# A four-stage transformer pipeline on one core: job 0's turn, the conditions and the table of places set anew

## What is computed

```python
# block 0: x += gate * self_attention(rope) ; x += gate * cross_attention ; x += gate * mlp(gelu)
mod = cond_global @ adaLN_W + adaLN_b                  # shifts, scales, gates
x_norm = _ln(x, norm1_w) * (1 + sc_msa) + sh_msa
q1, k1, v1 = qkv(x_norm[:, :n]); q2, k2, v2 = qkv(x_norm[:, n:])   # q, k turned by rope
self_out = _attn(q, k, v, attn_mask) @ attn_out_W
x = x + g_msa * self_out
...
# block 1: x += attention(ada_ln(x), ada_ln(ctx)) ; block 2: self attention, cross attention, mlp
# block 3: softmax attention over ctx, a router over three experts (silu), a gate, and the sum
```

## Time and profile before

| what | value |
|---|---|
| median of three runs | 637.37 us |
| the profiled execution, its own time | 639.46 us |
| its span | 637.7 us |
| PE busy | 560.0 us, 88% |
| DVE busy | 443.4 us, 70% |
| ACT busy | 407.7 us, 64% |
| POOL busy | 219.6 us, 34% |
| mean granted TensorE clock | 0.985 |

### The profile page before, as it was taken

How to read it: one execution, slowest core, us unless ns; L and a number is a source line. 1 busy time by engine, 2 the same in 40 slices (tenths; PEclk the granted TensorE clock), 3 DMA queues, 4 the chain that set the end, 5 groups by cost and what they waited for, 6 DMA issues and landing times.

```text
span 637.7 us, 25649 instructions
## 1 busy us (share of the span) xinstructions
PE 560.0 (88%) x11216; PEld 318.0 (50%) x11216; DVE 443.4 (70%) x1157; ACT 407.7 (64%) x704; POOL 219.6 (34%) x324
## 2 busy tenths in 40 slices
PE   6688977998779978898888988899999999998997
PEld 2344434445435545454544654465455655575456
DVE  5779877767896668768886878688676786244213
ACT  3233634675677447874788476868898868656762
POOL 6512442443541443523463344534342332110000
PEclk9999998999999979999998999999999999999999
DMA  6802000000000000000000000000000000000000
GB/s 207 320 4 68 20 2 19 19 2 20 19 20 3 20 1 21 17 3 19 21 18 2 5 18 18 2 20 4 19 4 2 4 3 19 4 3 19 3 3 35
DMA packets 15349, 16.32 MB, mean 26 GB/s; under 512 B 1830, under 2 KB 13108, under 8 KB 14856
## 3 DMA queue, kind: packets, MB, share of 16 engines
q1 hardware_dynamic: 14664, 10.70, 5.4%
q10 hardware_dynamic: 576, 4.00, 1.7%
HBM read 13.60 MB, written 1.09 MB: 23 GB/s over the span
## 4 chain that ended last, share of the span: by engine, by line
PE 56%; ACT 23%; DVE 13%; issue 5%; SPq 1%; POOL 1%; DMA 0%; DVEq 0%; POOLq 0%; ACTq 0%
PE lin L1027 17%; ACT P L639 14%; PE big L1027 11%; PE big L1190 9%; PE avp L1215 8%; PE big L1169 3%; DVE mhl L867 3%; PE big L1197 3%; ACT xn L603 2%; ACT L639 2%; PE lin L1119 1%; ACT L648 1%; ACT hid L648 1%; PE mtp L1027 1%; ACT hid L673 1%
## 5 line engine op out<-in xcount | busy, mean ns | idle before, releaser
L867 DVE TENSOR_REDUCE mhl<-big 128x8 bf16<-128x616 f32 (+1 forms) x160 | 149.4, 962 | 48.8 <-PE big L1169 46.7
L570 POOL TENSOR_TENSOR qm<-qT,hm 128x512 f32<-128x512 f32 x80 | 85.6, 1071 | 92.2 <-PE big L1197 49.8
L639 ACT ACTIVATE P<-big 128x1024 f32<-128x1024 f32 x64 | 62.0, 1021 | 69.4 <-PE big L1197 69.2
L1190 PE MATMUL big<-qm,kT 32*128 32x512 f32 x640 | 94.5, 661 | 0.0
L1215 PE MATMUL avp<-P,Vp 128*32 128x128 f32 x2560 | 90.4, 283 | 0.0
L556 POOL TENSOR_TENSOR kbm<-kT,hm 128x308 bf16<-128x308 f32 (+1 forms) x80 | 70.0, 874 | 51.0 <-PE big L1169 32.2
L533 POOL TENSOR_SCALAR rstd<-mv 128x4 f32<-128x4 f32 (+3 forms) x37 | 8.7, 234 | 218.6 <-DVE mv L816 218.3
L639 ACT ACTIVATE P<-big,padcol 128x1024 f32<-128x1024 f32 x64 | 67.8, 1110 | 25.0 <-PE big L1197 24.9
L1215 PEld LDWEIGHTS avp<-P,Vp 128*32 128x32 f32 x2560 | 71.8, 113 | 20.1 <-issue 17.2
L1027 PE MATMUL lin<-hT,W 128*32 128x512 f32 (+2 forms) x608 | 77.6, 589 | 0.2
L1169 PE MATMUL big<-kbm,qb 32*128 32x308 bf16 (+1 forms) x320 | 50.9, 332 | 23.0 <-ACT P L639 22.6
(11 more groups left out here) (208 smaller groups left out, 878.4 us busy)
## 6 DMA issues: line engine op xcount, KB each, us to landing
gring<-gate_rows SPq DMA_DIRECT2D x20, 256.0 KB, 3.2
W<-in_w ACTq DMA_DIRECT2D x2, 1152.0 KB, 14.0
hid<-in_ws SPq DMA_DIRECT2D x2, 768.0 KB, 5.8
W<-in_w ACTq DMA_DIRECT2D x1, 1088.0 KB, 9.1
x<-in_x SPq DMA_DIRECT2D x4, 256.0 KB, 6.8
out<-x SPq DMA_DIRECT2D x4, 256.0 KB, 2.4
ctx<-in_ctx SPq DMA_DIRECT2D x4, 154.0 KB
ctxT<-in_ctxT SPq DMA_DIRECT2D x4, 154.0 KB
```

Of the source, the lines that this page charges most:

```text
L570: nc.gpsimd.tensor_tensor(qm[:, j % 2], q.broadcast_to([128, 4, T]), mask.broadcast_to([128, 4, T]), ALU.mult).then_inc(qm_ready, 1)
L639: nc.scalar.activation(P[:, 8 * half:8 * half + 8, :], big[:, 2 * half:2 * half + 2, :].rearrange("p g (h q) -> p (g h) q", h=4), ACT.Exp, ...
L867: v.tensor_reduce(mhl[:].rearrange("p (g c) -> p g c", c=32)[:, 2 * half:2 * half + 2, 0:4], big[:, 2 * half:2 * half + 2, 0:4 * kw].rearr ...
L1190: mm(big[:, g, :].rearrange("p (h q) -> p h q", h=4), kT[s][r, b * kw:b * kw + 128], qm[r, j % 2], start=(a > 0), stop=False, skip_group_c ...
```

## The change

Of the table `SLOTS`, two of 45 rows are shown as samples; the others move by a few slots in the same manner, and the number and kind of units stay.

```diff
 SLOTS = {
...
-    (1, 0): [0, 3, 6],
+    (1, 0): [6, 7, 12],
...
-    (6, 0): [18],
+    (6, 0): [28],
...
-UNITS = ([("B", u, 0) for u in FIRST] + [("START", None, None)]
-         + [("B", u, 0) for u in (("p0", "k"), ("p0", "q"), ("p0", "v"))])
+UNITS = ([("B", u, 0) for u in FIRST] + [("START", None, None), ("B", ("p0", "k"), 0), ("A", 0, 0),
+                                         ("B", ("p0", "q"), 0), ("B", ("p0", "v"), 0)])
 for _slot in range(END):
-    UNITS.append(("A", _slot // 4, _slot % 4))
+    if _slot > 0:
+        UNITS.append(("A", _slot // 4, _slot % 4))
     UNITS += [("B", u, s) for slot, u, s in PLACED if slot == _slot]
-EARLY = [8, 12, 6, 6]
+EARLY = [8, 7, 2, 6]
...
                 v.tensor_scalar(sinT[:], sinT[:], turnsign[:], None, ALU.mult).then_inc(sign_set, 1)
+                v.tensor_scalar(mqk[:], mqk8[:], -1.0, BIG, ALU.add, ALU.mult)
+                v.tensor_scalar(mkq[:], mkq8[:], -1.0, BIG, ALU.add, ALU.mult).then_inc(masks_ready, 1)
+
+            def later_constants():
+
                 v.tensor_tensor(condr[:], condT[:].unsqueeze(2).broadcast_to([128, B, 3]),
                                 rw[:, 2:3, :].broadcast_to([128, B, 3]), ALU.mult)
-                for dst, src in ((mqk, mqk8), (mkq, mkq8), (mcb[:, 0:B * C], mc8)):
-                    i = v.tensor_scalar(dst[:], src[:], -1.0, BIG, ALU.add, ALU.mult)
-                chain(i)
-                v.memset(mhl[0:1, 0:1], 0.0).then_inc(consts_ready, 1)
+                v.tensor_scalar(mcb[:, 0:B * C], mc8[:], -1.0, BIG, ALU.add, ALU.mult).then_inc(consts_ready, 1)
...
             for kind, u, s in UNITS:
                 if kind == "START":
+                    later_constants()
                     for half in range(2):
                         maxima(0, half)
+                    turned(0)
                 elif kind == "A":
                     if s == 0:
-                        turned(u)
-                    if s == 0:
                         if u > 0:
+                            turned(u)
                             normalise(u - 1)
...
                 if part == "mods":
                     pe.wait_ge(silu_done, 1)
                     pe.wait_ge(ws_rest_in, 32)
+                    pe.wait_ge(consts_ready, 1)
...
                 if kind == "START":
                     keep_warm(EARLY[3])
-                    pe.wait_ge(consts_ready, 1)
+                    pe.wait_ge(masks_ready, 1)
```

More of the change, by code:

```diff
@@ L389, in build @@
             "cond_in", "ws_first_in", "ws_rest_in", "ident_in", "consts_in", "w_first_in", "w_rest_in"))
-        first_mods, consts_ready = sem("first_mods"), sem("consts_ready")
+        first_mods, masks_ready, consts_ready = sem("first_mods"), sem("masks_ready"), sem("consts_ready")
         gate_rows_out = sem("gate_rows_out")
```

## The result

| | before | changed |
|---|---|---|
| median of four runs each, same chip | 639.53 us (637.12 to 641.99) | 632.38 us (630.35 to 633.42) |
| ratio, 95% interval | | 0.9891 (0.9848 to 0.9934) |
| profiled execution, span | 639.46, 637.7 | 630.35, 628.5 |
| PE busy, mean granted clock | 560.0, 0.985 | 553.0, 0.993 |

What follows compares the result with a forecast made beforehand. It took PE and each job's own path to bound the kernel from job 4 on. Start 3.5 plus table 0.5 gave 4.0 us off 639.46: 635.5, expected as 633.4 for a run, range 629.3 to 638.0.

Steps and rivals of the forecast that it cites:

- Constants, 0.2 us by the lock: Set-up: condr and mcb leave the chain ahead of sample 0's rope but wait for GpSimd's qm; gain 0.2 us, bounds 0.2 to 0.85.
- Job 0's turn, job 1's copy at 28.9: First jobs: job 0's copy of turned maxima at 19.2 us instead of 23.89, job 1's at 28.9 instead of 36.76.
- The stall: PE's 3.34 us idle inside the conditions' matmuls, read as instructions delayed behind the weights; it goes in the new order.
- Conditions, job 2's copy at 40.4: Conditions and their tables now ahead of job 2's copy, uncovered; that copy at 40.4 us, 4.5 us earlier than before.
- Bias rows, cost 1.3 (0 to 1.8): On DVE behind job 3's copy: their 1.8 us partly fill 0.5 us of idle time, costing 1.3 us.
- First gates, "it just fits": SP's first gate loads behind the bias rows: land at 60.0 us, first used at 60.4; a miss costs its lateness.
- Start, 3.5 us: Set-up and first jobs together: 3.2 us earlier at job 4's copy, 3.5 us with the next window's lost copy of V.
- Table, 0.5 us: Moved units in jobs from 4 on: 0.5 us gained, an even shift of 5% of PE's 54 us idle being 2.7 us.
- The rival with this result (628.5): Table gives more than the start: PE's idle time in jobs 4 to 79 shrinks by a tenth, 5.4 us; chance 0.22.
- the absorbed gain: Rival: stall tied to the conditions returns 3.3 us and bias rows cost their full 1.8; 636.7 us, chance 0.15.
- The slower one: Rival: the granted clock falls several times before job 4, adding 5 us; 638.4 us, chance 0.08.
- Its own signs: Listed trace marks for right (five copy times, no long stall) and wrong (clock under 0.9, distance growing to 8 or 0).

Runs made afterwards that it cites:

- The experiment: Changed kernel with condr and mcb one step later on DVE, behind job 0's turned copy and k's rope: ratio 0.9864, median 631.9 us.
- start and conditions: Changed set-up and the conditions at slots 6, 7 and 12, other table rows as in the kernel before: 639.91 us, ratio 0.9991 to the kernel before.
- the table alone: Changed kernel's whole new table, conditions included, with the set-up of the kernel before: 635.53 us, ratio 0.9935 to the kernel before.
- the start alone: Changed set-up (UNITS, constants, EARLY) with the whole table of the kernel before: 638.58 us, ratio 0.9968 to the kernel before.

## Why the prediction was right, and where it was not

- *Idle matmuls, gain nothing:* right in total. In the trace above the clock did fall at 12.7 us, and the scores' mask took 1.04 us for 0.62, so the maxima waited 0.28 us for PE behind mcb; with the old idle matmuls job 0's copy came no earlier (19.15). (The counts go from 18 to 9, not from 20 to 11.)
- *Constants, 0.2 us by the lock:* 0.1 and 0.4 in the two traces, with condr stretched from 0.20 to 1.04. The experiment shows both sides: behind k's rope the whole gain is there (0.94). The bounds of 0.2 to 0.85 held nearly.
- *Job 0's turn, job 1's copy at 28.9:* 29.07 and 28.73.
- *The stall:* the reading as instructions that came late was right: it was tied to a count (twice shown), and its end came 1.3 us behind the packet's landing. That the weights held the packet up is not shown. "The stall then goes" was right for its 3.34 us. Missed: the next multiple, 962, gives a pause of 1.2 to 1.6 us in the same stretch, since PE runs the conditions' 256 records faster than the next packet comes; its 0.9 us on the gate rows lie in job 2's window.
- *Conditions, job 2's copy at 40.4:* 40.64 and 39.96.
- *"From job 2 to job 3 nothing else changes (9.68 us)":* failed. It took 10.47 us in both traces of the changed kernel, 0.8 more. All of it is DVE's wait for PE's k projection behind job 2's turn, and it comes with the moved conditions: 10.47 with start and conditions and with the table alone as well, 9.68 with the start alone. The start alone, then the changed kernel:

```profile
45.15 0.01 DVE L845 LOAD_MASK_SELECT oT<-lin  x1 [0.27 <-PE lin L1031]
```

```profile
43.28 0.01 DVE L845 LOAD_MASK_SELECT oT<-lin  x1 [1.05 <-PE lin L1031]
```

- *Bias rows, cost 1.3 (0 to 1.8):* job 3 to job 4 took 7.02 us, where 5.8 + 1.3 = 7.1 was forecast: right, with L887's 0.9 us in it.
- *First gates, "it just fits":* missed by 0.39 us.
- *Start, 3.5 us:* oversized. The changed kernel has 2.2 to 2.9 at job 4. But what this term counts is the start with the conditions and the old table otherwise, and that run had 1.6 us at job 4 and 0.6 in the median, with an interval that holds none. So 3.5 should have been 0 to 2.
- *Table, 0.5 us:* the mis-sized term. "An even shift of 5% either way" was put on PE's idle time, and that did not move (54.2 to 54.1). What moved there was the clock, which the term left out: before, PE's waits of 1.3 us ahead of the scores in jobs 10 and 28 stood ahead of falls at 106 and 229 us; the new table makes them 0.35. Measured, 4 us by the table alone and 5 to 7 as what it adds to the new start, some 3 of them at jobs 28 to 31 in the two traces. The rival with this result (628.5) was wrong in its mechanism as well: between jobs 4 and 79 no idle time was won.
- *The rivals:* the absorbed gain is out, by the stall's count. (Its sum is wrong too: 3.5 less 3.3 and less 0.5 for the bias rows is -0.3, not 0.2, and its time 637.2, not 636.7.) The slower one was wrong in its sign: one fall more in set-up did occur, covered, and over the whole run the clock gives back more than it takes.
- *Its own signs:* of those for right, the five copies came within 1.0 us, no stall of over 2 us came before 60 us, and condr was stretched; but the wait for gring came. Two of those for wrong came true as well: the clock was under 0.9 between 10 and 31 us (two falls of 3.4 us make 0.84), and the distance to the old copies grew to 7.8 us by job 79, which by the prediction's own words means that the table and not the start decides. It does.

The gain was 7 us and not 4, and its main part came from a place and by a mechanism that the forecast had put near nothing. The forecast time was still close by luck: the start was put too high and the table too low, and I had set the sum against the median shown then, 637.37, while the kernel before measured 639.53 in the comparison.

## What to carry to other kernels

Look at the granted clock per stretch before weighing idle time: a pause may cost once for itself and again, at the lower level, for the work behind it (here waits of 1.3 us, with 1.0 to 1.9 us behind them); filling it with work moved from elsewhere can earn both. Put the mean clock beside the time of each execution: it tells which part of a gain is the clock. A pause on "issue" in the middle of equal instructions can be a matter of their count: find it by counting all of the engine's records, look for the instruction packet that lands ahead of its end, and don't credit it to the code that stands there. It comes where many small instructions run faster than the next packet can arrive (256 records in under 2.5 us here). Moving a step off the path pays only as far as what takes its place; here moving the conditions gave 7 us at job 1 behind the old start and 5.6 behind the new one, and 1 us and nothing at job 4.

## What the runs showed of the hardware

- PE's pauses without a shown wait came at counts of its records a multiple of 256 apart (706, 962, 20930): 3.3 to 4.5 us while the weights were loading, 1.2 to 1.65 us between 35 and 39 us, 0.4 to 1.4 us in the last block, and mostly unseen between. All 29 ended 1.2 to 1.5 us behind the landing of a packet of 16,384 bytes on the instruction queue.
- A fall of the granted clock to its lower level cost 1.0 to 1.9 us in jobs 28 to 31. Two executions of one kernel had them at different places (the changed kernel at 12.7 and 26.4 us, the second time at 25.5, 97.2, 168.8 and 247.4), which is much of what separates such runs: over 167 executions 0.01 of the mean clock went with 4.3 us.
- A DVE product with two inputs of only 48 columns took as long as a whole GpSimd multiplication beside it, 1.04 us for 0.20.
